# Two transformer layers on one core: second-layer heads begin a slot sooner, the turn goes ahead of the output product, the FFN's output opens the sum's bank

## The reference

```python
xn = _layernorm(x)
x = x + L0_attn(xn) + L0_ffn(xn)      # 16 heads of 128, causal mask; gelu FFN, 1024 wide, fp8 products
xn = _layernorm(x)
x = x + L1_attn(xn) + L1_ffn(xn)      # 16 heads of 16, no mask; silu FFN, 1024 wide, Hadamard transforms
```

## Time and profile before

| what | value |
|---|---|
| median of 3 runs | 980.52 us (976.35 to 980.92) |
| profiled execution | 982.77 us, its span 980.7 us |
| mean granted TensorE clock | 0.977 |
| TensorE busy | 900.6 us, 92% |
| VectorE busy | 755.2 us, 77% |
| ScalarE busy | 680.5 us, 69% |
| GpSimd busy | 348.4 us, 36% |

### The profile page before, as it was taken

The page is one execution under the profiler, slowest core; times in us unless marked ns, Lnnn a source line. Parts: engine busy times, 40 slices in busy tenths (PEclk is TensorE's granted clock), DMA queues, the critical chain, the costliest instruction groups (busy, mean ns, idle before and its releaser), DMA issues.

```text
span 980.7 us, 22791 instructions
## 1 busy us (share of the span) xinstructions
PE 900.6 (92%) x7965; PEld 723.5 (74%) x8032; DVE 755.2 (77%) x2128; ACT 680.5 (69%) x1997; POOL 348.4 (36%) x637
## 2 busy tenths in 40 slices
PE   4877889899999999999999999999999999987797
PEld 2434667677788878888888888888888888866575
DVE  6787676667878887888788888888878887877576
ACT  4787687457767777777767776777677767776464
POOL 5502357334333333333333333333323333333243
PEclk9878999999999999999999999999999999999799
DMA  9242360002000200020002000100011000100000
GB/s 306 85 149 62 123 204 13 1 3 81 1 1 11 63 11 14 2 70 3 23 2 63 10 23 2 51 22 23 1 35 38 23 1 12 50 1 23 1 13 11
DMA packets 46879, 39.96 MB, mean 41 GB/s; under 512 B 4400, under 2 KB 42032, under 8 KB 46512
## 3 DMA queue, kind: packets, MB, share of 16 engines
q1 hardware_dynamic: 46768, 38.52, 12.8%
HBM read 30.11 MB, written 8.39 MB: 39 GB/s over the span
## 4 chain that ended last, share of the span: by engine, by line
PE 60%; DVE 17%; ACT 10%; issue 5%; POOL 0%; another core or an unknown queue 0%; ACTq 0%; DVEq 0%; POOLq 0%
PE ps L823 32%; PE ps L949 6%; ACT arena L1172 5%; DVE arena L816 5%; PE ps L872 4%; DVE arena L817 4%; PE ps L1048 3%; PE ps L1066 3%; ACT arena L812 3%; PE ps L845 3%; DVE arena L1332 3%; PE ps L1077 2%; PE ps L907 2%; PE ps L1050 1%; ACT arena L811 1%
## 5 line engine op out<-in xcount | busy, mean ns | idle before, releaser
L817 DVE SCALAR_TENSOR_TENSOR arena<-ps,bqk,arena 128x256 bf16<-128x256 f32 x416 | 187.5, 479 | 76.3 <-ACT arena L812 76.3
L812 ACT ACTIVATE arena<-ps,bqk 128x256 bf16<-128x256 f32 x416 | 177.9, 463 | 80.8 <-PE ps L1050 62.7
L816 DVE TENSOR_TENSOR arena<-ps,arena 128x512 bf16<-128x512 f32 (+1 forms) x336 | 204.1, 633 | 23.6 <-ACT arena L811 23.2
L823 PE MATMUL ps<-arena,wqkv 128*128 128x256 bf16 x1728 | 217.0, 277 | 2.5 <-DVE arena L816 2.5
L811 ACT ACTIVATE arena<-ps 128x512 bf16<-128x512 f32 (+1 forms) x336 | 180.8, 558 | 35.8 <-PE ps L872 21.4
L1563 POOL TENSOR_SCALAR arena<-arena,rc 128x128 f32<-128x128 f32 (+1 forms) x256 | 106.3, 429 | 272.6 <-DVE rc L1361 272.5
L1172 ACT ACTIVATE arena<-arena,nb 128x128 f32<-128x128 f32 (+1 forms) x256 | 114.4, 447 | 126.9 <-DVE nb L1332 126.8
L1570 POOL TENSOR_SCALAR arena<-arena,rc 128x256 f32<-128x256 f32 x254 | 119.0, 482 | 221.7 <-DVE rc L1365 221.7
L823 PEld LDWEIGHTS ps<-arena,wqkv 128*128 128x128 bf16 x1728 | 171.6, 99 | 26.9 <-issue 1.7
L1172 ACT ACTIVATE arena<-ps,nb 128x256 f32<-128x256 f32 x256 | 119.3, 478 | 20.3 <-DVE nb L1339 20.2
L823 PE MATMUL ps<-arena 128*128 128x128 bf16 (+2 forms) x864 | 98.9, 251 | 13.5 <-DVE arena L817 6.5
(11 more groups left out here) (115 smaller groups left out, 1278.5 us busy)
## 6 DMA issues: line engine op xcount, KB each, us to landing
scratch_qk<-arena SPq DMA_DIRECT2D x28, 128.0 KB, 1.9
arena<-scratch_qk SPq DMA_DIRECT2D x84, 32.0 KB, 1.8
arena<-scratch_qk SPq DMA_DIRECT2D x42, 64.0 KB, 2.5
arena<-in_x SPq DMA_DIRECT2D x4, 512.0 KB, 9.4
arena<-in_w_gating SPq DMA_DIRECT2D x4, 512.0 KB, 8.3
arena<-in_w_q SPq DMA_DIRECT2D x4, 512.0 KB, 4.6
arena<-in_w_k SPq DMA_DIRECT2D x4, 512.0 KB, 5.6
arena<-in_w_v SPq DMA_DIRECT2D x2, 1024.0 KB, 6.6
```

The costliest lines, as they stand in the source:

```text
L812: return nc.scalar.activation(out, in_, ACT.Identity, bias=bias)
L816: return nc.vector.tensor_tensor(out, in_, hi, ALU.subtract)
L817: return nc.vector.scalar_tensor_tensor(out=out, in0=in_, scalar=bias, in1=hi, op0=ALU.add, op1=ALU.subtract)
L823: last = nc.tensor.matmul(out, lhsT, rhs, start=(n == 0), stop=(n == len(steps) - 1))
```

## The change

- head_slot: the second-layer heads start at +11 instead of +12. In the last item but one, the table has one head in each of the slots +11 to +14 (123 to 126) and two in each from +15 (127) to +20 (132). quad_slot and out_slot follow by formula, and by new tables for that item.
- turn1_bank: a second head is turned in BK_QK if it is scored below slot 128, else in BK_S. turn1 gets two waits: in BK_QK also for the exponentials of the heads scored there so far, in BK_S for the q piece of the last item.
- Order: turn1 of first heads stands ahead of project_out0 on TensorE, p1_high ahead of p0_high on ScalarE, p1_low ahead of p0_low on VectorE.
- The sum's bank BK_X is opened by one matmul of identb by ybin (512 columns) at head 0 in place of ones by brow; the two matmuls at head 15 go. ybin is loaded a cycle sooner. The bias b_o of the first layer is added to rows by GpSimd (bias_rows0, slot 16b+17), and x1_sum waits for that. brow and the biases' parts are half as wide.

```diff
@@ slots
             if b == LASTB - 1:
-                return start1(b) + 12 + (0, 0, 1, 1, 2, 2, 3, 4, 4, 5, 5, 6, 6, 7, 7, 8)[h]
-            return start1(b) + 12 + h
+                return start1(b) + 11 + (0, 1, 2, 3, 4, 4, 5, 5, 6, 6, 7, 7, 8, 8, 9, 9)[h]
+            return start1(b) + 11 + h
...
-                return start1(b) + (15, 18, 21, 22)[q]
+                return start1(b) + (16, 18, 20, 22)[q]
...
-                return start1(b) + (16, 22, 22, 23)[q]
+                return start1(b) + (17, 19, 21, 23)[q]
...
-                    return BK_QK if head_slot(n) + 1 < NG0 else BK_S
+                    return BK_QK if head_slot(n) < NG0 else BK_S
@@ turn1
                 if bank == BK_QK:
                     pe.wait_ge(qk0_lo, min(slot + 1, NG0))
+                    scored = [m for m in range(B * H1) if score1_bank(m) == BK_QK and head_slot(m) <= slot]
+                    if scored:
+                        pe.wait_ge(exp1, scored[-1] + 1)
                 elif bank == BK_S:
                     pe.wait_ge(p0_lo, NG0)
+                    if slot >= piece_slot(3 * LASTB):
+                        pe.wait_ge(qkv1_lo, 3 * LASTB + 1)
@@ project_out0
-                if n == 0:
-                    pe.wait_ge(bias_rows, 1)
                 if h == 0:
-                    upto(pe, x1_done, b)
-                    open_bank(BK_X)
-                if h == H0 - 1:
                     if b == 0:
                         pe.wait_ge(f8_ready, 1)
                     pe.wait_ge(y_ready, 16 * (b + 1))
-                    for i in range(TT):
-                        nc.tensor.matmul(ps[:, BK_X, i * D:(i + 1) * D], identb[:, :], ybin[:, i, :], start=False,
-                                         stop=False)
+                    upto(pe, x1_done, b)
+                    nc.tensor.matmul(ps[:, BK_X, :], identb[:, :], ybin[:, :, :].rearrange("p i d -> p (i d)"),
+                                     start=True, stop=False)
@@ down
+                if n == 0:
+                    pe.wait_ge(bias_rows, 1)
                 if k == 0:
-                    open_bank(y_bank(b), True)
+                    open_y(y_bank(b))
@@ pe_program, slots below END (act_program and dve_program alike: p1_high, p1_low ahead of p0_high, p0_low)
                 if 0 <= s - 2 < NG0:
                     turn0(s - 2)
-                if 0 <= s - 4 < NG0:
-                    project_out0(s - 4)
                 for n in heads_in[s - 1]:
                     if not second(n):
                         turn1(n)
+                if 0 <= s - 4 < NG0:
+                    project_out0(s - 4)
@@ x1_sum
-                dve.wait_ge(rows_ready[b % 2], 16 * (b // 2 + 1))
+                dve.wait_ge(rows_biased, b + 1)
@@ pool_program
+            def bias_rows0(b):
+                if b == 0:
+                    pool.wait_ge(biases_loaded, 32)
+                pool.wait_ge(rows_ready[b % 2], 16 * (b // 2 + 1))
+                for i in range(TT):
+                    v = rows[:, b % 2, i, :]
+                    last = nc.gpsimd.tensor_tensor(v, v, bo_rows, ALU.add)
+                last.then_inc(rows_biased, 1)
...
+                if s % H0 == 1 and s > H0:
+                    bias_rows0(s // H0 - 1)
@@ sp_program
-                if b == 0:
-                    sp.wait_ge(y_stored, 16 * PAIRS)
-                upto(sp, out0_ps, H0 * b)
+                sp.wait_ge(y_stored, 16 * (b // 2 + 1))
+                if b:
+                    sp.wait_ge(out0_ps, H0 * (b - 1) + 1)
...
-                if g == 10 and b < B:
-                    load_y(b)
+                if s == 1:
+                    load_y(0)
+                if g == 10 and b + 1 < B:
+                    load_y(b + 1)
```

More of the change, by code:

```diff
@@ L64, in build @@
         ones = sb("ones", [P, P], BF16)
-        brow = sb("brow", [P, 2, 512], BF16)
+        brow = sb("brow", [P, 512], BF16)
         st = sb("st", [P, B * TT, 6], F32)
@@ L112, in build @@
             "p (r k t) -> p r k t", r=4, k=KD)
[L114 to L117, removed]
+        bo = sp0[:, 0, 0:D]
+        bo_hi = pt0[:, 0, 0, 0:D]
+        bo_rest = bias_room[:, D:2 * D]
+        bo_mid = oT0[:, 0, 0, :]
+        bo_rows = bias_room[:, 0:D]
         carve = carver(FIRST1)
@@ L326, in sp_setup @@
             load_x(3)
-            for w, name in enumerate(("bo0", "bo1")):
-                sp.dma_start(bo[:, w, :], t[name].partition_broadcast(P)).then_inc(biases_loaded, 16)
+            for place, name in ((bo_rows, "bo0"), (bo, "bo1")):
+                sp.dma_start(place, t[name].partition_broadcast(P)).then_inc(biases_loaded, 16)
             sp.dma_start(mask[:, :], t["mask"]).then_inc(consts_loaded, 16)
@@ L382, in pool_setup @@
             nc.gpsimd.memset(ones[:, :], 1.0)
-            nc.gpsimd.memset(brow[:, :, :], 0.0).then_inc(half_ready, 1)
+            nc.gpsimd.memset(brow[:, :], 0.0).then_inc(half_ready, 1)
             pool.wait_ge(half_ready, 2)
@@ L561, in dve_setup @@
                 for i in range(2):
-                    last = nc.vector.tensor_copy(brow[r:r + 1, :, i * D:(i + 1) * D], part[r:r + 1])
+                    last = nc.vector.tensor_copy(brow[r:r + 1, i * D:(i + 1) * D], part[r:r + 1])
             last.then_inc(bias_rows, 1)
@@ L787, in build @@
         norm0, norm1, rstd1, h1_lo = (sem(n) for n in ("norm0", "norm1", "rstd1", "h1_lo"))
-        rows_ready = [sem(f"rows_ready{i}") for i in range(2)]
+        rows_ready, rows_biased = [sem(f"rows_ready{i}") for i in range(2)], sem("rows_biased")
         spilled = [[sem(f"spilled_{w}{i}") for i in range(2)] for w in "qk"]
@@ L824, in group, with open_y @@
                 return last
-            def open_bank(bank, closing=False):
-                nc.tensor.matmul(ps[:, bank, :], ones[:, :], brow[:, int(bank != BK_X or closing), :], start=True,
-                                 stop=False)
+            def open_y(bank):
+                nc.tensor.matmul(ps[:, bank, :], ones[:, :], brow[:, :], start=True, stop=False)
             def scores0(n):
@@ L1275, in act_program @@
                     qk0_high(s)
+                for n in heads_in[s - 1]:
+                    if not second(n):
+                        p1_high(n)
                 if 0 <= s - 2 < NG0:
@@ L1279, in act_program @@
                     split_high(act, c, 0)
-                for n in heads_in[s - 1]:
-                    if not second(n):
-                        p1_high(n)
                 for n in heads_in[s]:
@@ L1504, in dve_program @@
                     qk0_low(s)
-                if 0 <= s - 2 < NG0:
-                    p0_low(s - 2)
                 for n in heads_in[s - 1]:
@@ L1509, in dve_program @@
                         p1_low(n)
+                if 0 <= s - 2 < NG0:
+                    p0_low(s - 2)
                 fold(s)
```

## The result

| | before | after |
|---|---|---|
| median (13 runs each) | 980.7 us (976.35 to 983.08) | 970.8 us (966.4 to 975.03) |
| ratio | | 0.9908, interval 0.9887 to 0.9929 |
| profiled execution, span | 982.77, 980.7 | 970.8, 968.9 |
| mean granted clock | 0.977 | 0.988 |

I had forecast 982.0 (973 to 989).

The account below looks back on a forecast made before the run. TensorE, busy 92%, was taken to bound six nearly full cycles, and chains through all engines the end. Terms of +6.8 and, for the end, -5.3 gave +1.5 on the median 980.5: 982.0 us, range 973 to 989.

Parts of the forecast that it names:

- The stall in slot 8: Slot 8 of six cycles: attend1 waits behind the k piece for its bank, 2.15 us each, plus 0.55 for attend1.
- What the order gives back: Full cycles: swapped turn and evictions partly close gaps before L1048; slots 9 and 10 -0.6, slots 12 to 15 -0.67 us.
- Rival C: Full cycles: all gaps close, 1.2 us more per cycle, six times, 975 us; chance 0.30 together with a hidden stall.
- The start: Bias rows' copies ahead of the first q/k eviction get half as wide: -0.4 us.
- The end: Slots 124 to 133: single heads in 124 to 126 give -6.7; with later gains and losses -5.3 us, bounds 0 and -9.
- The two waits of slot 128: Slot 128: TensorE idles 3 us after its scores, and turn1 of head 5 waits for exponentials in BK_QK.
- rival B: Slot 8 stalls: the clock falls, 1.4 us each; six times 990.4 us, half of them 986.2; chance 0.15.
- The bank: Sum's bank opened by one identity matmul per batch: 0.22 us less, eight times, seven where TensorE is full.
- The first stack: First cycle: earlier heads' operands from the k transfers arrive late by 0 to 1 us once, taken as +0.3.
- The bias on GpSimd: Two adds per batch on GpSimd, 0.67 us each, cost nothing; uncovered 1.3 us in slot 129 at most.

Follow-up runs that it names:

- the order alone: Kernel before with only turn1 ahead of project_out0 and p1_high, p1_low ahead of p0_high, p0_low: 969.41 us, ratio 0.9883.
- the slots alone: Kernel before with only the earlier head slots, new tables, banks of second heads and their two waits: 990.78 us, ratio 1.0101.
- the wait alone: Kernel before with one wait added, so that GpSimd's half of the wo split comes second, behind VectorE's: 976.73 us, ratio 0.9961.
- the bank alone: Kernel before with only the new opening of BK_X, the bias added by GpSimd and brow half as wide: 976.49 us, ratio 0.9946.
- order and bank: Kernel before with the new order and the new opening of the bank, heads in their old slots: 966.15 us, ratio 0.9857.
- late pairs: Kernel before with new order and bank, old slots, but the last item but one, from +12, pairs heads in +14 to +20: 962.77 us, ratio 0.9829.
- the old tables: Changed kernel with the former slot tables for the last item but one, starting at +12: 977.48 us, ratio 0.9951.
- two casts more: Changed kernel with two extra 1x256 casts on VectorE behind the bias copies: 973.78 us, ratio 0.9936.
- six casts: Changed kernel with six extra 1x256 casts on VectorE behind the bias copies: 973.54 us, ratio 0.9919.

## Why the prediction was wrong, step by step

- **The stall in slot 8: right.** Foreseen 2.15, measured 2.10, six times; with attend1 2.65 against 2.70.
- **What the order gives back: the step that failed in the cycles.** I put slots 9 and 10 at -0.6 and 12 to 15 at -0.67, with the argument that VectorE comes to the swapped L816 too late, so that only part of the gap closes. Measured -1.23 and -1.0, and -0.59 in slots 0 to 7, where I had only the bank's -0.22. That makes -1.49 foreseen, and -2.82 measured. In the changed kernel the L1048 of slots 8, 10, 11 and 15 start at

```profile
521.76 0.50 PE L1048 MATMUL ps<-arena 128*128 128x256 bf16 x3
...
532.94 0.49 PE L1048 MATMUL ps<-arena 128*128 128x256 bf16 x3
...
539.49 0.49 PE L1048 MATMUL ps<-arena 128*128 128x256 bf16 x3
...
562.19 0.49 PE L1048 MATMUL ps<-arena 128*128 128x256 bf16 x3 [0.22 <-DVE arena L817]
```

  From slot 8 to slot 10 it is 11.2 us, against 12.4 in the earlier trace rows, from slot 11 to slot 15 22.7 for 23.7. My error in slot 10: I held VectorE's chain fixed at 534.2, as if the work ahead of it stayed where it was. It starts as soon as TensorE's scores do, and they moved with the slot before (this reading is argued from the order in the slot; no run takes it apart). Rival C, that all gaps close, was the right one: it was worth 1.2 a cycle on my account, and 1.38 was measured. The runs show its cause: the order alone takes 1.82 off a cycle and leaves 0.07 of gap, the slots alone put 1.68 on, and the two together make -0.14, near the -0.17 measured (the bank's 0.23 adds nothing beside the order). A gap in front of a product was priced by the last wait ahead of it in one slot; the cycle's whole idle of 2.1 us was the better measure, and I had it only as a bound.
- **The start: the other step that failed.** I had the copies at -0.4, and they brought 0.54 (1.78 to 1.24). Not seen was what stands behind them: two engines starting 0.13 us apart on halves of one weight. The row with 3.07 us beside its neighbours of 1.22 was in the trace before, and I had read only the tile brow. Of the 6.6 us up to slot 4, 2.5 were there at 76 us already, and these I count as chance: the order alone, whose code is that of the kernel before up to there, was 3.2 ahead of it at the split. In the kernel before, the wait alone brought 4.4 in the median, the bank alone 4.6. So I put the change's share at about 4, an estimate.
- **The end: right in its large parts.** L1048 of slot 124's start to the scores of 127: foreseen 17.6, measured 17.55 (847.26 to 864.81). Turn1 of slot 129 behind those scores: foreseen 17.7, measured 17.68. The two waits of slot 128 are there, one as TensorE's wait of 2.5 for the maximum, one as turn1's for GpSimd's product:

```profile
874.02 0.52 PE L845 MATMUL ps<-ident,arena 128*128 128x128 f32 x3 [2.48 <-DVE nb L1334]
...
878.66 0.63 PE L877 MATMUL ps<-ident,arena 128*128 128x128 f32 x4 [1.65 <-POOL arena L1572]
...
882.49 0.63 PE L877 MATMUL ps<-ident,arena 128*128 128x128 f32 x4 [0.41 <-DVE arena L818]
```

  From there to the end I had +1.4, and it was -0.1. The row that bears on the difference is the clock's: the kernel before is at half for 10 us in the last stage, of which this is one stretch, and so were the six others whose last item but one begins at +12 (the bank, the order, GpSimd second, order and bank, late pairs, and the old tables in the changed kernel); the seven executions with it from +11 on had 3 to 7 us of it there or none. Why, no run shows.

```profile
915.00:918.40 3.40, 2.44 (x11) 1.58 (x10) 2.59 (x6) 2.10 (x6) 0.88 (x3) 0.50 0.00 0
```

- **The clock at the stalls (rival B): right in part.** I took none. In the changed kernel one of six stalls was followed by a fall (slot 89 took 7.57 for 5.91), in a second execution two, with the slots alone, with two casts more and with the old tables two each, with six casts more none: 9 of 36. The eight executions without the stall have no fall between slots 24 and 123. The stall of slot 88 before, and the stretch behind it:

```profile
620.50:623.90 3.40, 1.47 (x25) 0.95 (x23) 1.57 (x3) 0.98 (x3) 0.77 (x2) 0.99 0.01 1
623.90:627.30 3.40, 3.40 (x20) 2.54 (x20) 1.36 (x6) 1.16 (x4) 0.00 (x0) 0.51 0.45 124
```

  Each costs 1.5 to 1.7 us; dense products stand on both sides, so my reason against it (that it needs transposes ahead of it) fell. The Trainium skill, "TensorE: Matmul & The Clock Gate", section "Why this matters for your kernels", warns only of idle gaps between bursts that are longer than these 2.1 us: by it none should fall, and the traces disagree for 9 of the 36.
- **The bank:** -0.23 a cycle alone as foreseen, and nothing once the order had closed the gaps. **The first stack:** foreseen 0.3, no wait seen. **The bias on GpSimd:** 0.73 an add, off the path as foreseen.

In the profiled executions the sum of my terms missed by 13.3: 6.2 at the start, of which 2.5 by chance, 5.6 in the cycles (7.3 without the fall of the clock), 1.5 in the end. That a fall of the clock hid 1.7 of the miss in the cycles is luck.

## What to carry to other kernels

Where one engine is full but for small gaps, price an edit of the order by the whole idle time of a cycle, not by the last wait before one product: a gap that closes in one slot moves the chain of the next. Test the parts of a change alone; here one part (the order, -11.7) carried more than the whole, and a second (the slots, +9.7) lost more in the cycles than it gained in the end, until attend1 was moved away from the piece that fills its bank, 958.4 together. And before costing a small saving, look at what follows it on the other engines: 0.5 us of copies decided which of two engines came first, worth 4.4 in the kernel before (by the forced order) and not seen in the median of the changed one.

## What was not expected of the hardware

VectorE's and GpSimd's subtractions of two SBUF operands don't share, they exclude one another for a whole instruction. Alone they take 1.22 and 2.12 us. In 13 of the 14 traces they overlap, and the second one ends about its own time behind the end of the first, 1.08 where VectorE is second and 1.97 to 1.98 where GpSimd is. Four of them: VectorE at 88.19 behind GpSimd's 87.11 (1.08 later; before), at 86.05 behind 84.97 (1.08; six casts); GpSimd at 85.26 behind VectorE's 83.29 (1.97; after) and at 84.67 behind 82.70 (1.97; two casts: 81.49 + 3.18 behind 81.48 + 1.22). The Trainium skill, "SBUF — State Buffer", section "SBUF: two separate sides", says just that for a VectorE instruction with two SBUF inputs and a GpSimd one that reads SBUF: whichever begins first has the shared ports for the whole instruction, and the other blocks. The traces agree, by the 1.08 and 1.97 above. What it means for a schedule is that the time of 128x1024 on VectorE is 1.22 or 3.07, decided by a tenth of a microsecond, and with GpSimd 0.4 us behind it costs GpSimd only 0.7 (2.81 for 2.12).
